# One order of its own for each engine in the first stage of a four-stage kernel

## The reference

```python
# layer 0, attention block
xn = layer_norm(x) * ln1_scale + ln1_bias
q, k, v = xn @ wq, xn @ wk, xn @ wv                    # 16 heads of 16
phi_q, phi_k = relu(q) + 0.001, relu(k) + 0.001
kv  = cumsum(einsum('bshm,bshd->bshmd', phi_k, v), axis=1)
num = einsum('bshm,bshmd->bshd', phi_q, kv)
den = einsum('bshm,bshm->bsh', phi_q, cumsum(phi_k, axis=1))
x1 = (num / den[..., None]) @ wo + x
y  = x1 + gelu(layer_norm(x1) @ w1 + b1) @ w2 + b2
x  = layernorm(x + y)
# layer 0, quantised product (weights and rows on a 6-bit grid, blocks of 32)
x  = layernorm(x + mx_quantize(x) @ mx_quantize(weight).T + bias)
# layer 1, delta rule over chunks of 32 tokens: its inputs
q, k, v = (silu(causal_conv4(x @ W)) for W in (Wq, Wk, Wv))
beta = sigmoid(x @ Wb);  k = k / norm(k);  kb, vb = k * beta, v * beta
A   = where(strictly_lower, kb @ k.T, 0)               # 32 x 32 for each chunk and head
inv = solve_triangular(eye + A, eye, unit_diagonal=True)
```

## Time and profile before

| | |
|---|---|
| median of the runs (three) | 5134.18 us (5132.64 to 5137.41) |
| the profiled execution | 5120.81 us |
| its span in the profile | 5119.1 us |
| mean granted TensorE clock | 0.957 |
| busy: PE, VectorE, ScalarE, GpSimd | 4617.7, 4119.6, 2802.1, 2775.1 us |

### The profile page before, as it was taken

How to read it: one execution, slowest core, us unless ns; L and a number is a source line. 1 busy time by engine, 2 the same in 40 slices (tenths; PEclk the granted TensorE clock), 3 DMA queues, 4 the chain that set the end, 5 groups by cost and what they waited for, 6 DMA issues and landing times. The chain is left out here.

```text
span 5119.1 us, 116501 instructions
## 1 busy us (share of the span) xinstructions
PE 4617.7 (90%) x42012; PEld 3868.0 (76%) x42012; DVE 4119.6 (80%) x12689; ACT 2802.1 (55%) x6469; POOL 2775.1 (54%) x3719
## 2 busy tenths in 40 slices
PE   5999999999999999999999939969999999999969
PEld 4887877877887787788788738947777777777745
DVE  4789889988888988888898852239999999999961
ACT  2554555555555555555555522137777777777751
POOL 1344444443444444444344423229999999999980
PEclk9999999999999999999999969979999999999979
DMA  1121222222122122112212237743444444444410
GB/s 44 42 62 51 62 59 59 58 65 60 47 63 66 51 62 63 55 58 64 59 48 65 60 78 164 181 123 113 121 116 116 121 114 118 120 114 120 118 60 27
DMA packets 738175, 416.03 MB, mean 81 GB/s; under 512 B 341764, under 2 KB 725576, under 8 KB 737608
## 3 DMA queue, kind: packets, MB, share of 16 engines
q1 hardware_dynamic: 667144, 372.92, 25.7%
q10 hardware_dynamic: 65664, 16.78, 1.4%
q0 software_dynamic: 4800, 18.88, 1.2%
HBM read 220.98 MB, written 187.43 MB: 80 GB/s over the span
## 5 line engine op out<-in xcount | busy, mean ns | idle before, releaser
L636 POOL TENSOR_TENSOR a_shift<-a_mean_var,a_eps 128x2 f32<-128x2 f32 x256 | 71.7, 280 | 1418.1 <-DVE a_mean_var L918 1418.1
L932 DVE SCALAR_TENSOR_TENSOR a_cv<-a_raw,a_taps,a_cv 128x256 f32<-128x256 f32 x1152 | 566.9, 564 | 10.1 <-DVE a_scaled L864 9.9
L1151 PE MATMUL a_bank<-a_turned,a_w 128*128 128x256 f32 x2048 | 455.9, 381 | 4.8 <-ACT a_turned L719 4.8
L1053 PE MATMUL a_bank<-a_w,a_hidden 128*128 128x256 f32 x2048 | 452.8, 379 | 0.9 <-ACT a_hidden L764 0.9
L1151 PEld LDWEIGHTS a_bank<-a_turned,a_w 128*128 128x128 f32 x2048 | 383.9, 190 | 59.1 <-ACT a_turned L719 8.8
L1053 PEld LDWEIGHTS a_bank<-a_w,a_hidden 128*128 128x128 f32 x2048 | 384.1, 190 | 51.3 <-ACT a_hidden L764 1.7
L1738 POOL TENSOR_TENSOR c_stats<-c_l2sq,half 128x16 f32<-128x16 f32 x128 | 374.7, 2927 | 73.0 <-DVE c_l2sq L1912 73.0
L1745 POOL TENSOR_TENSOR c_expd<-c_e,c_logit 128x16 f32<-128x16 f32 x128 | 371.6, 2903 | 0.0
L897 DVE TENSOR_TENSOR a_masked<-a_bank,keep_causal 128x512 f32<-128x512 f32 x512 | 317.5, 682 | 61.2 <-PE a_bank L1109 59.7
L2063 PE MATMUL c_bank<-c_u,c_grams 128*32 128x64 f32 (+2 forms) x3072 | 232.3, 219 | 57.4 <-ACT c_u L1784 57.3
L780 ACT ACTIVATE a_raw<-a_bank 128x512 f32<-128x512 f32 x192 | 114.9, 598 | 300.4 <-PE a_bank L1044 300.4
(11 more groups left out here) (291 smaller groups left out, 13094.0 us busy)
## 6 DMA issues: line engine op xcount, KB each, us to landing
a_x<-in_x SPq DMA_DIRECT2D x64, 256.0 KB, 3.0
scratch_xb<-a_xb SPq DMA_DIRECT2D x64, 256.0 KB, 2.1
scratch_xbT<-a_turned SPq DMA_DIRECT2D x128, 128.0 KB, 2.2
scratch_qT<-a_cv SPq DMA_DIRECT2D x128, 128.0 KB, 2.2
scratch_v<-a_qkv_rows SPq DMA_DIRECT2D x64, 256.0 KB, 2.2
scratch_kn<-a_kn SPq DMA_DIRECT2D x64, 256.0 KB, 2.1
scratch_vb<-a_qkv_rows SPq DMA_DIRECT2D x64, 256.0 KB, 2.1
scratch_kT<-a_kT SPq DMA_DIRECT2D x128, 128.0 KB, 2.6
```

The lines of the kernel that those rows point to most:

```text
L932: ins = dve.scalar_tensor_tensor(cv[s][:, n, c], raw[s][:, n, c, j:j + TOK], taps[:, n, c, j:j + 1], cv[s][:, n, c], ALU.mult, ALU.add)
L1053: ins = pe.matmul(dst[:, t * D:(t + 1) * D], src[s][:, c, tile_cols(t)], weight[:, c], start=(c == 0), stop=(c == chunks - 1))
L1151: ins = pe.matmul(dst[:, at:at + TOK], w1_sb[:, c, m * P:(m + 1) * P], x1nT[s][:, c], start=(c == 0), stop=(c == C - 1))
```

## The change

The single order gives way to a table for each engine, of the time at which each entry starts there, and each engine's queue is sorted by its own table. `PERIOD` (44.20) is in the same unit as the starts. The bank plan follows PE's order. Beside that:

- `qkv`, `mlp1`, `mlp2`, `qkv1` and `qkvT`, which were one entry each on PE, are entries for each product (`q`, `k`, `v`; `mlp10` to `mlp13`; `mlp20`, `mlp21`; `raw0` to `raw2`; `qkvT0` to `qkvT2`), so that others can stand between them. VectorE's features of q and k become two entries.
- Attention has a bank for each tile of 128 tokens (`attn0`, `attn1`), 38 uses of a bank a step, and ScalarE evacuates it in two halves of 128 x 2 x 128. The semaphore `masked_used` is gone.
- The inversion stays on VectorE, in the same pieces. The instructions themselves, their shapes and buffers, are otherwise the same.

```diff
-    PERIOD = 10.437
+    PERIOD = 44.20
...
-    shares = [("load", 1.52), ("ln1_stats", 0.73), ("ln1", 3.18), ("xnT", 4.13), ("qkv", 1.6), ("cum", 1.28),
...
+    starts = {
+        "sp": {"load": 0.00, "lnB": 143.23, "xbT": 151.95, "qkvT": 199.15, "kT": 220.43, "gram": 223.75,
+               "keep": 227.58, "gather": 231.70, "inverse3": 382.01},
...
     run = partial(run_pipelined, written=WRITTEN)
-    order = pipelined(shares, STEPS, sum(share for _, share in shares) / PERIOD)
+    order = {eng: interleaved(own, STEPS, PERIOD) for eng, own in starts.items()}
...
-    plan = PsumPlan(order, jobs_of, banks.count, batches)
+    plan = PsumPlan(order["pe"], jobs_of, banks.count, batches)
...
+            def attention(i, s):
+                for t in range(T):
+                    src = full(act, i, s, f"attn{t}")[:].rearrange("p (c n) -> p c n", c=C)
+                    freed(act.activation(attnT[s][:, :, tile_cols(t)], src[:, :, tile_cols(t)], ACT.Copy), s, f"attn{t}")
...
-                        if t == 0:
-                            dve.wait_ge(S["masked_used"], seq(i, s) - 1)
-                        else:
-                            computed(dve, *back(i, s, 1), "attn")
+                        computed(dve, *back(i, s, 1), f"attn{t}")
...
-            def attention(i, s):
-                dst = open_bank(i, s, "attn", "v", *(f"scores0{r}" for r in range(STRIPS)))
-                for t in range(T):
+            def attention(t):
+                def stage(i, s):
+                    dst = open_bank(i, s, f"attn{t}", "v", *(f"scores{t}{r}" for r in range(STRIPS)))
...
             def wo(i, s):
-                token_major(i, s, "wo", wt["wo"], attnT, "attn")
+                in_sbuf(pe, i, s, "attn0")
+                token_major(i, s, "wo", wt["wo"], attnT, "attn1")
```

More of the change, by code:

```diff
@@ L292, in phase_a @@
     GELUS = M // PER_BANK
-    shares = [("load", 1.52), ("ln1_stats", 0.73), ("ln1", 3.18), ("xnT", 4.13), ("qkv", 1.6), ("cum", 1.28),
[L296 to L301, removed]
+    starts = {
+        "sp": {"load": 0.00, "lnB": 143.23, "xbT": 151.95, "qkvT": 199.15, "kT": 220.43, "gram": 223.75,
+               "keep": 227.58, "gather": 231.70, "inverse3": 382.01},
[5 rows of a table added]
+               "gram": 225.44},
+        "act": {"ln1": 7.05, "xnT": 16.43, "v": 23.04, "den": 25.96, "phikT": 26.53, "rdenT": 37.55, "attn": 52.31,
+                "ln2": 73.51, "x1nT": 76.66, "mlp1": 84.23, "lnA": 118.77, "xdT": 133.06, "lnB": 141.86,
+                "xbT": 150.64, "qkv1": 165.75, "beta": 171.52, "qkvT": 195.38, "squares": 200.40, "kT": 222.04},
+        "dve": {"ln1_stats": 4.08, "q": 19.39, "k": 21.10, "cum": 22.00, "den": 25.39, "dS": 28.90, "rdenT": 30.07,
+                "scores0": 40.38, "scores1": 44.14, "wo": 68.64, "ln2_stats": 69.88, "mlp2": 105.19,
+                "lnA_stats": 105.84, "quant": 120.53, "ffn": 137.57, "lnB_stats": 138.92, "conv": 184.01,
+                "squares": 207.52, "keep": 226.77, "inverse0": 371.93, "inverse1": 373.61, "inverse2": 380.17,
+                "inverse3": 381.19},
+        "pool": {"ln1_stats": 5.25, "ln2_stats": 71.05, "x1nT": 72.64, "lnA_stats": 111.87, "lnA": 120.16,
+                 "lnB_stats": 140.09, "powers": 209.86},
+    }
@@ L302, in phase_a @@
     run = partial(run_pipelined, written=WRITTEN)
-    order = pipelined(shares, STEPS, sum(share for _, share in shares) / PERIOD)
+    order = {eng: interleaved(own, STEPS, PERIOD) for eng, own in starts.items()}
     jobs_of = {
-        "xnT": ["xnT"], "qkv": ["q", "k", "v"], "den": ["den"], "phikT": ["phikT"], "dS": ["dS"], "rdenT": ["rdenT"],
+        "xnT": ["xnT"], "q": ["q"], "k": ["k"], "v": ["v"], "den": ["den"], "phikT": ["phikT"], "dS": ["dS"], "rdenT": ["rdenT"],
         "scores0": [f"scores0{r}" for r in range(STRIPS)], "scores1": [f"scores1{r}" for r in range(STRIPS)],
[L307 to L310, removed]
-    }
@@ L312, in phase_a @@
-    plan = PsumPlan(order, jobs_of, banks.count, batches)
+        "attn0": ["attn0"], "attn1": ["attn1"], "wo": ["wo"],
+        "x1nT": ["x1nT"], "mlp20": ["mlp2"],
+        "xdT": ["xdT"], "ffn": ["ffn"], "xbT": ["xbT"],
+        "beta": ["beta"], "kT": ["kT"], "gram": ["G0", "G1"],
+    }
+    jobs_of |= {job: [job] for job in [f"mlp1{j}" for j in range(GELUS)] + [f"{n}{j}" for n in ("raw", "qkvT") for j in range(3)]}
+    plan = PsumPlan(order["pe"], jobs_of, banks.count, batches)
     HEADS, HEAD = 4, D // 4
@@ L693, in _ @@
             link = Chain(pool, S["pool_chain"])
-            run(pool, order, batches, stages, link, links)
+            run(pool, order["pool"], batches, stages, link, links)
         @block.scalar
@@ L832, in _, with features @@
             }
-            run(act, order, batches, stages)
+            run(act, order["act"], batches, stages)
         @block.vector
         def _(dve):
-            def features(i, s):
-                for job, dst in (("q", phiq), ("k", phik)):
+            def features(job, dst):
+                def stage(i, s):
                     src = full(dve, i, s, job)
@@ L842, in features @@
                     freed(ins, s, job)
+                return stage
             def key_sums(i, s):
@@ L1008, in _ @@
             link = Chain(dve, S["dve_chain"])
-            run(dve, order, batches, stages, link, links)
+            run(dve, order["dve"], batches, stages, link, links)
         @block.tensor
```

71 lines of the change are left out of this document (42 added, 29 removed), and 5 rows, old and new, of the table starts.

## The result

| | before | changed |
|---|---|---|
| median of the runs (4 each, side by side) | 5133.4 us | 5105.2 us |
| ratio, 95% interval | | 0.9945 [0.9927, 0.9962] |
| span of the profiled execution | 5119.1 us | 5098.8 us |
| mean granted clock | 0.957 | 0.961 |

The change gains 28 us where 181 were forecast. The time lies 108 us above the forecast's own range (4907 to 4997) and 40 us above the range given for 8 in 10 (4885 to 5065).

What follows compares the result with a forecast made beforehand. It took TensorE and VectorE, neither full, handing work back and forth in one order, as the bound. Steps from 45.7 to 42.4 us gave 55 x 3.3 = 181 us, first steps and draining cancelling: 4940 profiled, 4953 median, range 4907 to 4997.

Steps and rivals of the forecast that it cites:

- I price that meeting at 1 us, one blocked add: GpSimd's residual additions beside VectorE's inversion end and state additions cost VectorE 1 us a step, bounds 0 to 2.7.
- 40.2 us, under TensorE's 41.2: VectorE's 38.2 us of work plus 2.0 of gaps a step stays below TensorE's own work.
- VectorE's sum, 38.2 us: VectorE's busy time a step: 40.5, less 3.3 for collisions at the convolution and inversion adds, plus 1.0 for the meeting.
- TensorE's waits: Waits from walking one step in TensorE's new order: 0.5 us light, up to 3 heavy, taken as 1.2.
- TensorE's own work, 41.2 us: TensorE's time for a step at full clock without waits, read from a 42.2 us step holding waits of 0.77 and 0.29.
- Bank for each half: One more bank use a step for attention's halves shifts all banks, counted as 0 to 0.8 us in TensorE's waits.
- Load of x: hidden, without slack: Load queued behind stores kn and vb; its loop of 41.2 to 42.6 us is mostly hidden under TensorE's 42.4.
- First steps -8, draining +8: The five steps before the inversion gain 8 us in all; draining the pipeline loses 8 us (0 to 20).
- Rival 1: VectorE and the load of x set the pace, steps of 43.3 to 44.3 us, 5002 to 5057 us; chance 0.24.
- Rival 2: GpSimd's wide instructions collide with VectorE wherever put, VectorE at 45.6 us a step, 5129 us, no change; chance 0.06.
- Rival 3: TensorE stops at scores1 for banks and loses its clock, 47.2 to 48.7 us a step, 5217 to 5299; chance 0.09.
- Rival 4: No waits and no collisions, TensorE at 41.2 us a step, 4886 us; chance 0.09.

Runs made afterwards that it cites:

- e11: Changed kernel with only GpSimd's x1nT residual additions (L660, L661) moved behind the powers, L669 left beside the inversion: 4960.8 us, 0.9677 of the kernel before.
- e1: Changed kernel with GpSimd's residual additions x1nT and lnA (L660, L661, L669) moved behind the powers, beside VectorE's masked scores: 4928.8 us, 0.9591 of the kernel before.
- e4: Changed kernel with six extra matmuls of constants on TensorE ahead of its wait for xd, in two of four steps: 5061.3 us, 0.9851 of the kernel before.
- e2: Changed kernel with the load of the next x issued ahead of the stores of coef, kn and vb on the sync queue: 5102.9 us, 0.9931 of the kernel before.
- e5: Changed kernel with both GpSimd residual additions moved behind the powers and the load of x issued ahead of the stores: 4923.8 us, 0.9597 of the kernel before.
- e10: Single old order with split entries and a bank per attention half (5065.1 us), x1nT's additions moved earlier on GpSimd: 5108.7 us, 0.9958 of the kernel before.

## Why the prediction was wrong

- *"I price that meeting at 1 us, one blocked add (bounds 0, and 2.7 for both met in full)."* This is the step that failed. It measured 2.76 us, just over the upper bound. The price of a blocked instruction was about right (0.95 us from the earlier trace rows; 2.76 for three); the count was wrong, for there are three in a row. With only L669 left to meet VectorE, e11 has VectorE at 37.9 us (38.2 forecast), its step at 42.8 (42.4) and the kernel at 4960.8 us (4953).
- *"40.2 us, under TensorE's 41.2."* The size alone does not explain the time. With 2.76 in place of 1 the same sum gives VectorE 40.5 - 3.3 + 2.76 + 2.0 = 42.0 us, still under the 42.4 of the forecast, and a step took 45.4. The comparison adds up each engine for itself; what set the step was the loop through both, VectorE's 25.3 us from features to xd and TensorE's 21.9 from xd to the next features. VectorE's gaps, taken at 2.0 us, were 45.4 - 40.1 = 5.3.
- *VectorE's sum, 38.2 us.* It is 40.1: 1.8 of the 1.9 between them are the price of the meetings. The convolution at 7.2 us was right.
- *TensorE's waits, "together 0.5 in a light step, up to 3 in a heavy one; I take 1.2", and "I expect the clock near 1.00".* The four longest lines of its list (the two shown, 11.0 for a transposed tile, 3.3 for the scaled products) make 108.4 / 44 = 2.5 us a step. The walk had nothing for xd, whose wait alone is 1.6. It comes with the first item (e1 has none), but the walk should have had it as what is late next. The clock was 0.98; e4, with it back at 1.00, takes 44 us less.
- *TensorE's own work, 41.2 us.* In e1, with the clock at 1.00, it is busy 2290.07 / 55 = 41.6 us and idle 0.6: the forecast's 42.4 and e1's 42.3 agree partly by luck, for the first term was 0.4 short and the waits were priced 0.6 too high.
- *Bank for each half, "I count 0 to 0.8 in TensorE's waits".* The sign was wrong. It was counted as a cost, and it was a gain: about 64 us in the old order (1.2 a step), 16 in the new (0.3).
- *Load of x: hidden, without slack.* Hidden is right: e2 and e5 change nothing that can be told. The load lands in 3.8 us (median) behind the stores, for 3.0 before and 2.9 in e2: 0.8 more, where the prediction worked out 0.6.
- *First steps -8, draining +8.* Right: 9.0 less and 8.9 more.
- *Rival 1*, VectorE setting the pace with its meetings in full, came nearest: of its signs a blocked add showed, and the wait for the load stayed at 0.9 us a step. It was priced at 44.3 us a step, 1.1 too low; e4, with the clock restored, has 44.7. The load, its other half, had no part.
- *Rival 2*, GpSimd colliding wherever it is put, fell in the new order (e1) and stood in the old one (e10).
- *Rival 3*, a long wait before scores1 and the low clock behind it, has its second half in the traces: a wait of up to 2.6 us stands just there, for xd and not for a bank, and the scores behind it take 2.09 us for 1.15. *Rival 4*, 41.2 us a step, was reached by no run.

## What to carry to other kernels

When wide GpSimd instructions are moved, lay their whole run beside VectorE's queue. Here, in a stretch where every VectorE instruction reads two operands from SBUF, VectorE got one instruction done for each of GpSimd's, so count every meeting of the run and not one. Then look for a stretch in which VectorE reads PSUM and put them there; here two numbers in a table were worth 3.5%. Don't compare engines by their sums alone: follow the handing over from one to the other and back until the loop closes, and compare its length with the step. And price a late engine at the next wait of its partner, for behind the long waits the partner's clock fell here, and a microsecond of VectorE cost up to 1.6 of the step.

## What the runs showed of the hardware

- A GpSimd addition of 128x512 nearly keeps its own duration when it meets VectorE (1.27 to 1.39 us in the rows shown, for 1.26 to 1.28 beside the masked scores), while VectorE's product and add of 128x198 go from 0.35 and 0.37 us to 1.3: nearly all of the loss is VectorE's.
- VectorE's masked scores (one operand in PSUM) run beside the same additions at their full pace, 2.48 us for four; so does a product of 128x256 with one operand in PSUM (0.41 us beside L669), where a sum of two in SBUF takes 1.09 for 0.43.
- Six matmuls of constants in TensorE's wait of about 2.5 us, in two of every four steps, brought the granted clock of the middle piece from 0.98 to 1.00 and took 44 us off the kernel.
